# The third block's mixture of experts with two experts side by side

## The chip, the cores and the metric

The kernel runs on one core of a Trainium2 chip. The metric is the device time of one execution in microseconds (us). Three executions of the kernel before were timed; the median is the time before.

## What is computed

The reference is a network of four blocks, each of a cross attention, an attention or scan and a feed-forward part, on an x of 16 x 64 rows and 256 features. The kernel runs them as twelve layers, one after the other. The change concerns one, the feed-forward part of the block L2 (the third), whose layer is named `l2f`:

```
probs = softmax(x @ gate_w.T)            # 8 experts
topw, sel = top_k(probs, 2); topw /= sum(topw)
combine[t, e] = topw where e is selected, else 0
g, u = split(x @ w1[e].T)                # 176 and 176 columns
act = silu(g) * u
out = sum over e of combine[:, e] * (act @ w2[e].T)
```

Here x is the normalised stream and out is added to the stream. All eight experts are computed for every row; the weight of an expert that wasn't selected is zero. All of it is in fp32.

## The kernel before

`l2_ffn` (L3460) has the stream in SBUF as 8 tiles of 128 rows. A loop on each engine makes 4 trips, and each trip works on two tiles, called A and B here, whose programs are interleaved step by step (`in_turn`, L64): step i of A, then step i of B. There is no scheduler: the order of an engine's work is the order in which these programs are written, and semaphores carry the waits. Each tile has four PSUM banks: `hb` (two, for what the up-projection gives), `tb` (for transposed activations) and a bank for y.

A trip begins with a layer norm, its two transposes (L242), the gate's logits (L264, 8 columns), an exponential on POOL (L3497) and the choice of the two best on DVE (`Moe.route`, L613). POOL also splits a weight of the next layer into three bf16 parts after it, beside the experts (`ThreeParts.some`, L3609).

Then come the experts, in class `Moe` (L592). In `Moe.tensor` (L635) step i, 0 to 9, issues for each tile

- the up-projection of expert i (`project`, L264): 2 matmuls of 352 columns into `hb[i % 2]`, once DVE has read expert i-2 from it (signal `act_ready`);
- the transposes of expert i-1's 176 activations (L649), as parts of 128 and 48 columns, into `tb`, once DVE has made them and ACT has read the expert before from `tb` (`actT_ready`);
- the products of expert i-2 with `w_out` (L655), one matmul of 256 columns for each part, which contract over 128 and 48 rows and add up in y over all experts.

In `Moe.scalar` (L659) ACT computes the SiLU of the gate half (L665) and copies each transposed part to SBUF (L671). In `Moe.vector` (L673) DVE multiplies the other half by the SiLU and by the expert's weight (L680, into `act`, one of two buffers). `self.parts` holds the parts:

```
self.parts = [(a, min(P, inner - a)) for a in range(0, inner, P)]   # inner = 176
```

The trip ends with DVE's addition of y to the stream (L3518). The next trip's norm follows it.

The weights are loaded a layer ahead by SP (`l2_ffn_loads`, L3452), while layer `l2a` before runs. `w_out` comes in two transfers, rows 0 to 127 and 128 to 175 of every expert.

## Time and profile before

| | |
|---|---|
| median of 3 executions | 3598.69 us |
| lowest and highest | 3598.42 and 3602.27 us |
| the profiled execution | 3597.89 us |
| its span, from the first to the last instruction | 3596.1 us |
| mean granted TensorE clock | 0.876 |
| PE busy over the span | 2895.3 us (81%) |
| DVE, ACT, POOL busy | 2264.0, 1480.0, 588.4 us |

PE is TensorE's matmuls, PEld its weight loads, DVE VectorE, ACT ScalarE, POOL GpSimd, SP the engine that issues DMAs. "Idle before" is the time that the engine stood still before an instruction, with the one that ended the wait behind the arrow. An instruction can leave more than one record in the trace. PE's durations overlap at their ends, since matmuls are pipelined: what one costs in a full stream is the distance from its start to the start of the next. PEclk is the clock that TensorE was granted, as a share of 2.4 GHz, so 0.50 is 1.2 GHz.

### The profile page before, as it was taken

To read this page: it belongs to the slowest core of one execution; us is meant where nothing else is said; L and a number is where in the kernel's file an instruction comes from. 1 tells how busy PE (TensorE), PEld (TensorE's weight loads), DVE (VectorE), ACT (ScalarE), POOL (GpSimd) and SP (SyncE) were. 2 spreads that over 40 slices of the span, in tenths; PEclk is the share of its full clock that TensorE was granted. 3 is DMA by queue.
4 is the path that set the end of the run, shared out by engine and by line. 5 is a ranking of instruction groups with operands and counts; after the bars stand their busy time and mean duration, and the time that the engine had idled before them with its cause. 6 is when DMAs were issued, how large, how long until landed. Compare 5 with 4: busy or idle time off the path is not lost. (4 is left out here: it accounts for less than half of the span.)

```text
span 3596.1 us, 63959 instructions
## 1 busy us (share of the span) xinstructions
PE 2895.3 (81%) x24052; PEld 2020.0 (56%) x24100; DVE 2264.0 (63%) x4833; ACT 1480.0 (41%) x3050; POOL 588.4 (16%) x934
## 2 busy tenths in 40 slices
PE   6776699977867877749996869789999978787777
PEld 3333488776645555525654335456556557666666
DVE  6999644433658888776564832367777764444754
ACT  4899511112454645344442122155555533222222
POOL 5222100000002222111110032221211211111000
PEclk8899799988977778669998978899999989889788
DMA  4999900000010000010002040000000002000000
GB/s 121 198 204 206 215 0 0 0 24 6 15 53 3 3 2 3 2 75 6 9 9 72 2 140 23 3 4 3 3 6 3 3 27 116 1 0 0 1 1 12
DMA packets 316501, 141.44 MB, mean 39 GB/s; under 512 B 296221, under 2 KB 305950, under 8 KB 312613
## 3 DMA queue, kind: packets, MB, share of 16 engines
q1 hardware_dynamic: 308072, 138.46, 16.1%
q10 hardware_dynamic: 8256, 0.52, 0.2%
q8 instruction: 126, 2.06, 0.2%
q14 instruction: 47, 0.39, 0.0%
HBM read 67.65 MB, written 3.15 MB: 20 GB/s over the span
## 5 line engine op out<-in xcount | busy, mean ns | idle before, releaser
L1251 ACT ACTIVATE l0x_pb<-l0x_ex,l0x_neg_max,l0x_q_scale 128x2048 uint16<-128x2048 f32 x128 | 267.1, 2088 | 36.3 <-POOL l0x_neg_max L1354 25.0
L1150 PE MATMUL l0x_s_ps<-l0x_kT,l0x_qT 128*128 128x512 bf16 x466 | 167.0, 441 | 86.3 <-DVE l0x_ex L1449 42.8
L1447 DVE TENSOR_SCALAR_CACHE_REDUCE l0x_ex<-l0x_s_ps 128x1024 f32<-128x1024 f32 x128 | 156.3, 1221 | 15.2 <-PE l0x_s_ps L1150 14.5
L1449 DVE TENSOR_SCALAR_CACHE_REDUCE l0x_ex<-l0x_s_ps 128x1024 f32<-128x1024 f32 x128 | 156.2, 1221 | 0.0
L1150 PEld LDWEIGHTS l0x_s_ps<-l0x_kT,l0x_qT 128*128 128x128 bf16 x512 | 33.9, 102 | 155.6 <-DVE l0x_ex L1449 105.1
L264 PE MATMUL l3x_bank<-l3x_w_kv_x,l3x_ctxT 128*128 128x512 f32 x256 | 117.4, 601 | 4.4 <-ACT l3x_ctx_q L765 3.7
L2229 PEld LDWEIGHTS l1a_bank<-l1a_u,l1a_gm 64*64 64x64 f32 x2048 | 95.8, 193 | 17.7 <-issue 17.1
L1160 PEld LDWEIGHTS l0x_o_ps<-l0x_v,l0x_vT 128*128 128x128 f16 x2048 | 71.4, 99 | 60.6 <-DMA l0x_vT<-l0x_pb 30.3
L2229 PE MATMUL l1a_bank<-l1a_u,l1a_gm 64*64 64x8 f32 x2048 | 98.5, 235 | 7.7 <-DVE l1a_gm L2582 7.7
L264 PE MATMUL l2f_bank<-l2f_w,l2f_ln_yT 128*128 128x352 f32 x256 | 104.3, 542 | 0.0
L2221 PE MATMUL l1a_bank<-l1a_r,l1a_r 32*64 32x64 f32 x2048 | 70.9, 278 | 40.2 <-DVE l1a_r L2563 35.1
L2221 PEld LDWEIGHTS l1a_bank<-l1a_r,l1a_r 32*64 32x64 f32 x2048 | 65.0, 159 | 58.3 <-DVE l1a_r L2563 39.6
L680 DVE SCALAR_TENSOR_TENSOR l2f_moe_act<-l2f_bank,l2f_moe_cw,l2f_moe_sg 128x176 f32<-128x176 f32 x64 | 25.0, 400 | 115.5 <-ACT l2f_moe_sg L665 114.9
L710 PE MATMUL l3x_bank<-ident,l3x_rows 128*128 128x128 f32 x448 | 69.7, 289 | 33.3 <-ACT l3x_rows L758 33.3
L3714 PE MATMUL l3x_bank<-l3x_wproj,l3x_cat 128*128 128x256 bf16 x768 | 91.6, 277 | 4.1 <-DVE l3x_cat L3586 4.1
L2210 PE MATMUL l1a_bank<-l1a_steps,l1a_after 128*128 128x512 f32 x128 | 89.7, 790 | 0.0
L1160 PE MATMUL l0x_o_ps<-l0x_v,l0x_vT 128*128 128x16 f16 x2048 | 72.4, 171 | 18.9 <-DMA l0x_vT<-l0x_pb 18.6
L3714 PEld LDWEIGHTS l3x_bank<-l3x_wproj,l3x_cat 128*128 128x128 bf16 x768 | 74.4, 99 | 20.9 <-issue 6.6
L1351 POOL TENSOR_SCALAR l0x_mx<-l0x_low_max,l0x_high_max,l0x_q_neg 128x1 f32<-128x1 f32 x128 | 47.5, 371 | 216.2 <-DVE l0x_ex L1449 200.1
L4194 DVE TENSOR_TENSOR l3a_cur<-l3a_ret,l3a_bank 128x256 f32<-128x256 f32 x16 | 6.7, 422 | 117.7 <-PE l3a_bank L264 117.7
L710 PEld LDWEIGHTS l3x_bank<-ident,l3x_rows 128*128 128x128 f32 x448 | 51.0, 145 | 52.7 <-ACT l3x_rows L758 47.2
L655 PE MATMUL l2f_bank<-l2f_w,l2f_moe_actT 128*128 128x256 f32 (+1 forms) x256 | 78.6, 407 | 0.0
(756 smaller groups left out, 7774.9 us busy)
## 6 DMA issues: line engine op xcount, KB each, us to landing
l2f_wproj_raw<-in_L_xattn_wproj SPq DMA_DIRECT2D x2, 2048.0 KB, 12.8
l3a_w<-in_L_attn_W SPq DMA_DIRECT2D x4, 1024.0 KB, 10.6
l2f_w<-in_L_ffn_w SPq DMA_DIRECT2D x1, 2816.0 KB, 11.3
l0x_ex<-in_ctxT SPq DMA_DIRECT2D x8, 256.0 KB, 4.9
l0a_wq<-in_L_attn_W_Q SPq DMA_DIRECT2D x1, 2048.0 KB
l0a_wk<-in_L_attn_W_K SPq DMA_DIRECT2D x1, 2048.0 KB
l0x_vT<-l0x_pb SPq DMA_TRANSPOSE x128, 4.7
l0a_wv<-in_L_attn_W_V SPq DMA_DIRECT2D x1, 2048.0 KB, 7.9
```

The costliest lines, as they stand in the source:

```text
L264: ins = nc.tensor.matmul(out, wT(c), rhs(c), start=start and n == 0, stop=stop and n == chunks - 1)
L655: ins = nc.tensor.matmul(self.y, self.actT[0:w, e % 2, n, :], self.w_out[0:w, e, n, :], start=(e == 0 and n == 0), stop=(e == E - 1 and n ...
L710: ins = self.L.nc.tensor.transpose(self.banks[u][:, h * P:(h + 1) * P], self.rows[:, 4 * u + h, :], self.L.env.ident[:])
L1150: ins = mm(s_ps[:, j * 512:(j + 1) * 512], qT[:, h, :], kT[:, h // 2, j * 512:(j + 1) * 512], start=True, stop=True)
L1160: ins = mm(o_ps[:, h * HD:(h + 1) * HD], pt[:, h % 4, j * P:(j + 1) * P], vv[:, j, h * HD:(h + 1) * HD], start=j == 0, stop=j == KT - 1)
L1251: s.activation(pb[:, h % 4, :], ex[:, h % 4, :], ACT.Exp, scale=q_scale[:, h:h + 1], bias=nb[:, h:h + 1], accum_out=sums[:, h:h + 1]).then ...
L1447: v.tensor_scalar(ex[:, h % 4, 0:1024], s_ps[:, 0:1024], 1.0, None, ALU.mult, ALU.max, accum_out=low_max[:, h:h + 1]).then_inc(o.up(scores ...
L1449: v.tensor_scalar(ex[:, h % 4, 1024:2048], s_ps[:, 1024:2048], 1.0, None, ALU.mult, ALU.max, accum_out=high_max[:, h:h + 1]).then_inc(o.up ...
L2210: ins = mm(bank[4 + j][:], after[:], flat(steps_[:, 8 * j:8 * j + 8, :]), start=False, stop=True)
L2221: mm(out, r1[0][r, 8 * half + j, tok], r1[1][r, 8 * half + j, tok], start=True, stop=False)
L2229: ins = mm(bank[6][r, h * HP:(h + 1) * HP], gm[r, h, :], u[r, h * HP:(h + 1) * HP], start=True, stop=True)
L3714: ins = nc.tensor.matmul(y_bank, cat[:, 8 * (n % 2) + c, :], wproj[:, 8 * n + c, i, :], start=n % 2 == 0 and c + i == 0, stop=n % 2 == 1 a ...
```

## The change

Two experts with their 2 x 176 = 352 activations side by side are one row of 352 columns, cut into parts of 128, 128 and 96. DVE writes expert e into half e % 2 of a row of `act`, the buffers of `act` change with the pair instead of the expert. PE transposes at the even steps (2, 4, 6, 8) the pair that DVE has finished, three transposes for each tile, and multiplies by `w_out` at the odd steps (3, 5, 7, 9), three products for each tile. ACT copies the first two transposed parts in one instruction of 256 columns and the third in a second one. `w_out` is laid out on the host for pairs, three rows of 128 per pair with the last padded by zeros, and loaded in one transfer of 1,536 KB. The up-projections, SiLUs and DVE's products per expert are the same in number and size.

```diff
--- before.py
+++ after.py
@@ -597,17 +597,17 @@
         self.L, self.E, self.I, self.xT, self.w_in, self.w_out = L, experts, inner, xT, w_in, w_out
         self.hb, self.tb, self.y = banks[0:2], banks[2], y_bank
         self.fixed, self.factor = fixed, factor
-        self.parts = [(a, min(P, inner - a)) for a in range(0, inner, P)]
+        self.parts = [(a, min(P, 2 * inner - a)) for a in range(0, 2 * inner, P)]
         self.score = L.sb(f"{name}_score", [P, 8])
         self.top, self.idx = L.sb(f"{name}_top", [P, 8]), L.sb(f"{name}_idx", [P, 8], mybir.dt.uint32)
         self.idxf, self.iota = L.sb(f"{name}_idxf", [P, 8]), iota
         self.second, self.den = L.sb(f"{name}_second", [P, 8]), L.sb(f"{name}_den", [P, 1])
         self.cw = L.sb(f"{name}_cw", [P, 8 + fixed])
-        self.sg, self.act = L.sb(f"{name}_sg", [P, 2, inner]), L.sb(f"{name}_act", [P, 2, inner])
+        self.sg, self.act = L.sb(f"{name}_sg", [P, 2, inner]), L.sb(f"{name}_act", [P, 2, 2 * inner])
         self.actT = L.sb(f"{name}_actT", [P, 2, len(self.parts), P])
         E = experts
         self.hid_ps, self.silu = L.sig(f"{name}_hid_ps", E), L.sig(f"{name}_silu", E)
-        self.act_ready, self.actT_ps, self.actT_ready = L.sig(f"{name}_act_ready", E), L.sig(f"{name}_actT_ps", E), L.sig(f"{name}_actT_ready", E)
+        self.act_ready, self.actT_ps, self.actT_ready = L.sig(f"{name}_act_ready", E), L.sig(f"{name}_actT_ps", E // 2), L.sig(f"{name}_actT_ready", E // 2)
         self.y_ps = L.sig(f"{name}_y_ps")
 
     def route(self, o):
@@ -640,20 +640,20 @@
                 if i >= 2:
                     pe.wait_ge(self.act_ready.sem, self.act_ready.value(t, i - 1))
                 project(nc, self.hb[i % 2][:, 0:2 * I], lambda c: self.xT[:, c, :], lambda c: self.w_in[:, c, i * 2 * I:(i + 1) * 2 * I], DC).then_inc(self.hid_ps.sem, 1)
-            if 1 <= i <= E:
-                e = i - 1
-                pe.wait_ge(self.act_ready.sem, self.act_ready.value(t, e + 1))
-                if e:
-                    pe.wait_ge(self.actT_ready.sem, self.actT_ready.value(t, e))
+            if i >= 2 and i % 2 == 0:
+                pair = i // 2 - 1
+                pe.wait_ge(self.act_ready.sem, self.act_ready.value(t, 2 * pair + 2))
+                if pair:
+                    pe.wait_ge(self.actT_ready.sem, self.actT_ready.value(t, pair))
                 for n, (a, w) in enumerate(self.parts):
-                    ins = nc.tensor.transpose(self.tb[0:w, n * P:(n + 1) * P], self.act[:, e % 2, a:a + w], self.L.env.ident[:])
+                    ins = nc.tensor.transpose(self.tb[0:w, n * P:(n + 1) * P], self.act[:, pair % 2, a:a + w], self.L.env.ident[:])
                 ins.then_inc(self.actT_ps.sem, 1)
-            if i >= 2:
-                e = i - 2
-                pe.wait_ge(self.actT_ready.sem, self.actT_ready.value(t, e + 1))
+            if i >= 3 and i % 2:
+                pair = i // 2 - 1
+                pe.wait_ge(self.actT_ready.sem, self.actT_ready.value(t, pair + 1))
                 for n, (a, w) in enumerate(self.parts):
-                    ins = nc.tensor.matmul(self.y, self.actT[0:w, e % 2, n, :], self.w_out[0:w, e, n, :],
-                                           start=(e == 0 and n == 0), stop=(e == E - 1 and n == len(self.parts) - 1))
+                    ins = nc.tensor.matmul(self.y, self.actT[0:w, pair % 2, n, :], self.w_out[0:w, pair, n, :],
+                                           start=(pair == 0 and n == 0), stop=(2 * pair == E - 2 and n == len(self.parts) - 1))
         ins.then_inc(self.y_ps.sem, 1)
 
     def scalar(self, o):
@@ -663,12 +663,13 @@
             if i < self.E:
                 o.eng.wait_ge(self.hid_ps.sem, self.hid_ps.value(o.t, i + 1))
                 s.activation(self.sg[:, i % 2, :], self.hb[i % 2][:, 0:I], ACT.Silu).then_inc(o.up(self.silu), 1)
-            if 1 <= i <= self.E:
-                e = i - 1
-                o.eng.wait_ge(self.actT_ps.sem, self.actT_ps.value(o.t, e + 1))
-                for n, (a, w) in enumerate(self.parts):
-                    last = n == len(self.parts) - 1
-                    s.activation(self.actT[0:w, e % 2, n, :], self.tb[0:w, n * P:(n + 1) * P], ACT.Copy).then_inc(o.up(self.actT_ready if last else None), 1)
+            if i >= 2 and i % 2 == 0:
+                pair = i // 2 - 1
+                o.eng.wait_ge(self.actT_ps.sem, self.actT_ps.value(o.t, pair + 1))
+                whole_rows = len(self.parts) - 1
+                s.activation(flat(self.actT[:, pair % 2, 0:whole_rows, :]), self.tb[:, 0:whole_rows * P], ACT.Copy).then_inc(o.up(), 1)
+                w = self.parts[-1][1]
+                s.activation(self.actT[0:w, pair % 2, whole_rows, :], self.tb[0:w, whole_rows * P:(whole_rows + 1) * P], ACT.Copy).then_inc(o.up(self.actT_ready), 1)
 
     def vector(self, o):
         v, I = self.L.nc.vector, self.I
@@ -677,7 +678,7 @@
             if e >= self.E:
                 continue
             o.eng.wait_ge(self.silu.sem, self.silu.value(o.t, e + 1))
-            v.scalar_tensor_tensor(out=self.act[:, e % 2, :], in0=self.hb[e % 2][:, I:2 * I], scalar=self.cw[:, e:e + 1], in1=self.sg[:, e % 2, :],
+            v.scalar_tensor_tensor(out=self.act[:, e // 2 % 2, e % 2 * I:(e % 2 + 1) * I], in0=self.hb[e % 2][:, I:2 * I], scalar=self.cw[:, e:e + 1], in1=self.sg[:, e % 2, :],
                                      op0=ALU.mult, op1=ALU.mult).then_inc(o.up(self.act_ready), 1)
 
 
@@ -3446,15 +3447,14 @@
 
 def l2_ffn_weights(W):
     E, I = 8, 176
-    return (W.sb("w1", [P, DC, E * 2 * I]), W.sb("w2", [P, E, 2, D]), W.sb("gate_w", [P, DC, E]), W.sb("iota", [P, 8]))
+    return (W.sb("w1", [P, DC, E * 2 * I]), W.sb("w2", [P, E // 2, 3, D]), W.sb("gate_w", [P, DC, E]), W.sb("iota", [P, 8]))
 
 
 def l2_ffn_loads(sp, d, W, w1, w2, gate_w, iota):
     sp.dma_start(gate_w[:], d["L2_ffn_gate_w"]).then_inc(W.sem, W.loaded())
     sp.dma_start(iota[:], d["iota8"]).then_inc(W.sem, W.loaded())
     sp.dma_start(w1[:], d["L2_ffn_w1"]).then_inc(W.sem, W.loaded())
-    sp.dma_start(w2[:, :, 0, :], d["L2_ffn_w2a"]).then_inc(W.sem, W.loaded())
-    sp.dma_start(w2[0:176 - P, :, 1, :], d["L2_ffn_w2b"]).then_inc(W.sem, W.loaded())
+    sp.dma_start(w2[:], d["L2_ffn_w2"]).then_inc(W.sem, W.loaded())
 
 
 def l2_ffn(nc, env):
@@ -4753,8 +4753,9 @@
         f["L2_attn_" + n] = spread(i["L2_attn_" + n])
 
     f["L2_ffn_gate_w"], f["L2_ffn_w1"] = rows(i["L2_ffn_gate_w"].T), rows(i["L2_ffn_w1"].reshape(-1, D).T)
-    w2 = i["L2_ffn_w2"].transpose(2, 0, 1)
-    f["L2_ffn_w2a"], f["L2_ffn_w2b"] = np.ascontiguousarray(w2[:P]), np.ascontiguousarray(w2[P:])
+    w2 = np.zeros((4, 3 * P, D), np.float32)
+    w2[:, 0:2 * 176] = i["L2_ffn_w2"].transpose(0, 2, 1).reshape(4, 2 * 176, D)
+    f["L2_ffn_w2"] = np.ascontiguousarray(w2.reshape(4, 3, P, D).transpose(2, 0, 1, 3))
 
     g = lambda n: i["L3_xattn_" + n]
     for n in ("wq", "wk", "wv", "wqx", "w_kv_x", "wproj"):
```

PE at the start of a trip's experts (L264 the up-projection, x2 for one expert and tile; L649 a transpose; L655 a product with `w_out`; ISA and REGISTER_ALU rows set registers of a wait). Before:

```order
L264 MATMUL l2f_bank<-l2f_w,l2f_ln_yT 128x352 x6
L645 ISA
L649 MATMUL l2f_bank<-ident,l2f_moe_act 128x128
L649 MATMUL l2f_bank<-ident,l2f_moe_act 48x128
L264 MATMUL l2f_bank<-l2f_w,l2f_ln_yT 128x352 x2
L649 MATMUL l2f_bank<-ident,l2f_moe_act 128x128
L649 MATMUL l2f_bank<-ident,l2f_moe_act 48x128
L264 MATMUL l2f_bank<-l2f_w,l2f_ln_yT 128x352 x2
L645 REGISTER_ALU
L649 MATMUL l2f_bank<-ident,l2f_moe_act 128x128
L649 MATMUL l2f_bank<-ident,l2f_moe_act 48x128
L655 MATMUL l2f_bank<-l2f_w,l2f_moe_actT 128x256 x2
```

The same place after the change:

```order
L264 MATMUL l2f_bank<-l2f_w,l2f_ln_yT 128x352 x8
L641 ISA
L264 MATMUL l2f_bank<-l2f_w,l2f_ln_yT 128x352 x2
L645 REGISTER_ALU
L649 MATMUL l2f_bank<-ident,l2f_moe_act 128x128 x2
L649 MATMUL l2f_bank<-ident,l2f_moe_act 96x128
L264 MATMUL l2f_bank<-l2f_w,l2f_ln_yT 128x352 x2
L649 MATMUL l2f_bank<-ident,l2f_moe_act 128x128 x2
L649 MATMUL l2f_bank<-ident,l2f_moe_act 96x128
L264 MATMUL l2f_bank<-l2f_w,l2f_ln_yT 128x352 x2
L653 ISA
L655 MATMUL l2f_bank<-l2f_w,l2f_moe_actT 128x256 x3
```

Before, three up-projections (x6) stand ahead of the first wait for DVE, and the fourth, B's second, behind A's first transposes. Now four (x8) stand ahead of it, and six transposes of a step stand with two up-projections between products.

PE at the close of a trip, from B's last products of the step before on. Before:

```order
L655 MATMUL l2f_bank<-l2f_w,l2f_moe_actT 128x256 x2
L645 REGISTER_ALU
L649 MATMUL l2f_bank<-ident,l2f_moe_act 128x128
L649 MATMUL l2f_bank<-ident,l2f_moe_act 48x128
L655 MATMUL l2f_bank<-l2f_w,l2f_moe_actT 128x256 x2
L649 MATMUL l2f_bank<-ident,l2f_moe_act 128x128
L649 MATMUL l2f_bank<-ident,l2f_moe_act 48x128
L655 MATMUL l2f_bank<-l2f_w,l2f_moe_actT 128x256 x6
```

After the change:

```order
L655 MATMUL l2f_bank<-l2f_w,l2f_moe_actT 128x256 x3
L645 REGISTER_ALU
L649 MATMUL l2f_bank<-ident,l2f_moe_act 128x128 x2
L649 MATMUL l2f_bank<-ident,l2f_moe_act 96x128
L649 MATMUL l2f_bank<-ident,l2f_moe_act 128x128 x2
L649 MATMUL l2f_bank<-ident,l2f_moe_act 96x128
L653 REGISTER_ALU
L655 MATMUL l2f_bank<-l2f_w,l2f_moe_actT 128x256 x6
```

Before, the products of the expert before stand between a tile's last transposes and its last products. Now only the other tile's three transposes stand there.

## Rows read from the trace of the kernel before

**Rows 1.** Stretches of the expert stage: us, busy (records) per engine, PEclk, DMA, GB/s.

```profile
2157.75:2198.78 41.03, 41.03 (x148) 23.15 (x148) 6.19 (x16) 11.13 (x46) 5.77 (x4) 0.95 0.13 51
...
2169.41:2180.05 10.64, 10.64 (x42) 6.08 (x41) 1.60 (x4) 2.60 (x12) 0.00 (x0) 1.00 0.07 28
2090.00:2316.00 226.00, 197.38 (x688) 114.59 (x688) 65.83 (x192) 56.14 (x208) 69.81 (x56) 0.87 0.15 56
```

**Rows 2.** Groups by line and shape: records, busy us, mean ns, idle before.

```profile
L264 PE MATMUL l2f_bank<-l2f_w,l2f_ln_yT 128*128 128x352 f32 x256 | 104.3, 542 | 0.0
L655 PE MATMUL l2f_bank<-l2f_w,l2f_moe_actT 48*128 48x256 f32 x128 | 44.5, 428 | 0.0
L655 PE MATMUL l2f_bank<-l2f_w,l2f_moe_actT 128*128 128x256 f32 x128 | 39.0, 387 | 0.0
L649 PE MATMUL l2f_bank<-ident,l2f_moe_act 128*128 128x128 f32 x64 | 18.9, 295 | 13.9 <-DVE l2f_moe_act L680 13.9
```

**Rows 3.** Timeline of PE, second trip: start, duration, instructions, idle before.

```profile
2144.87 0.69 PE L242 MATMUL l2f_bank<-ident,l2f_ln_y 128*128 128x128 f32 x2 [0.25 <-DVE l2f_ln_y L213]
2145.35 1.77 PE L264 MATMUL l2f_bank<-l2f_gate_w,l2f_ln_yT 128*128 128x8 f32 x8
2146.97 6.20 PE L264 MATMUL l2f_bank<-l2f_w,l2f_ln_yT 128*128 128x352 f32 x12
2157.75 0.69 PE L649 MATMUL l2f_bank<-ident,l2f_moe_act 128*128 128x128 f32 x2 [4.58 <-DVE l2f_moe_act L680]
2158.23 2.55 PE L264 MATMUL l2f_bank<-l2f_w,l2f_ln_yT 128*128 128x352 f32 x4
...
2166.75 1.45 PE L264 MATMUL l2f_bank<-l2f_w,l2f_ln_yT 128*128 128x352 f32 x4
...
2168.26 1.22 PE L655 MATMUL l2f_bank<-l2f_w,l2f_moe_actT 128*128 128x256 f32 x4
2169.41 1.45 PE L264 MATMUL l2f_bank<-l2f_w,l2f_ln_yT 128*128 128x352 f32 x4
...
2193.34 0.44 PE L649 MATMUL l2f_bank<-ident,l2f_moe_act 128*128 128x128 f32 x2
...
2195.05 3.73 PE L655 MATMUL l2f_bank<-l2f_w,l2f_moe_actT 128*128 128x256 f32 x12
2202.09 0.69 PE L242 MATMUL l2f_bank<-ident,l2f_ln_y 128*128 128x128 f32 x2 [3.31 <-DVE l2f_ln_y L213]
```

**Rows 4.** Timeline of PE, first trip.

```profile
2103.35 1.35 PE L264 MATMUL l2f_bank<-l2f_w,l2f_ln_yT 128*128 128x352 f32 x4
2104.53 0.38 PE L649 MATMUL l2f_bank<-ident,l2f_moe_act 128*128 128x128 f32 x2
2104.75 1.22 PE L655 MATMUL l2f_bank<-l2f_w,l2f_moe_actT 128*128 128x256 f32 x4
```

**Rows 5.** Timeline of DVE, second trip.

```profile
2157.29 1.02 DVE L680 SCALAR_TENSOR_TENSOR l2f_moe_act<-l2f_bank,l2f_moe_cw,l2f_moe_sg 128x176 f32<-128x176 f32 x3
```

**Rows 6.** Timeline of ACT, second trip.

```profile
2144.65 0.39 ACT L251 ACTIVATE l2f_ln_yT<-l2f_bank 128x256 f32<-128x256 f32 x1 [5.52 <-PE l2f_bank L242]
...
2193.82 0.43 ACT L671 ACTIVATE l2f_moe_actT<-l2f_bank 128x128 f32<-128x128 f32 x2 [0.99 <-PE l2f_bank L649]
```

**Rows 7.** Timeline of the DMA issues on SP's queue.

```profile
1952.10 7.19 SPq L3457 DMA_DIRECT2D l2f_w<-in_L_ffn_w2b  x1
2065.27 1.72 SPq L3219 DMA_DIRECT2D l2a_turn_out<-l2a_res  x2
```

**Rows 8.** DMA issues by size, us to landing.

```profile
l2f_w<-in_L_ffn_w2b SPq DMA_DIRECT2D x1, 384.0 KB, 16.5
```

**Rows 9.** PE in single microseconds: busy (records), PEclk, DMA, GB/s.

```profile
2157.00:2158.00 1.00, 0.25 (x1) 0.50 0.00 0
...
2162.00:2163.00 1.00, 1.00 (x6) 0.96 0.00 0
...
2201.00:2202.00 1.00, 0.00 (x0) 0.50 0.00 0
```

## The prediction

> **What bounds the kernel here.** The change touches one stage of twelve, the mixture of experts of the third block, so the first view is the table of stretches over that stage. It lies between 2090 and 2316 us of the span; in these 226 us PE is busy 197.4, DVE 65.8, ACT 56.1, POOL 69.8 [rows 1]. Inside the steady part of one trip, 2169.41 to 2180.05, PE is busy 10.64 of 10.64 us at full granted clock, ACT 2.60 and DVE 1.60. PE sets the pace and nothing else is near it, so what PE no longer issues is worth its issue time.
>
> The second view, groups by line and shape, tells what PE issues [rows 2]. Each fp32 matmul of the source leaves two records, each transpose leaves one. So there are 128 up-projections (352 columns), 128 products with w_out (256 columns; half of them contract over 48 rows), and 128 transposes (half of 48 columns). The 48-row products are no cheaper than the 128-row ones, 428 ns against 387 a record. An expert of 176 columns pays for two full blocks: that is the waste the change goes for.
>
> The third view is PE's timeline. In the steady part one expert of one tile has a period of 2166.75 to 2169.41 = 2.66 us [rows 3]. Its pieces at full clock: two up-projections (call them **h**) 2103.35 to 2104.53 = 1.18, two transposes 2104.53 to 2104.75 = 0.22 [rows 4], so 0.11 each (**t**), and the two products take the rest, 2.66 - 1.18 - 0.22 = 1.26, so 0.63 each (**o**). These add up over a whole trip: from 2157.75 to 2198.78 the second trip issues 13 h, 32 t and 32 o, which is 15.34 + 3.52 + 20.16 = 39.0, and half of the 4.3 us that it spends at half clock (below) makes it 41.2; the stretch is 41.03 us [rows 1].
>
> **The change part by part.**
>
> *Fewer PE instructions.* A pair of experts had 4 transposes and 4 products per tile; it now has 3 and 3. With 8 tiles and 4 pairs, 32 t and 32 o go: 32 x 0.11 + 32 x 0.63 = 3.5 + 20.2 = **-23.7 us**. Bounds: an o in the mixed pattern could be as little as 1.15/2 = 0.575 (2168.26 to the next period at 2169.41), which makes it 21.9 in all. The up-projections and the SiLUs and DVE products per expert stay as they are.
>
> The new third transpose has 96 columns where the one removed had 48. The rows: at half clock a pair of one full and one 48-column transpose takes 2157.75 to 2158.23 = 0.48, and a pair of two full ones (the norm's) 2144.87 to 2145.35 = 0.48 [rows 3]. So the width of the loaded block doesn't count and three cost 0.33. The Trainium skill speaks against that ("TensorE: Matmul & The Clock Gate", section "LDWEIGHTS (loading the stationary operand)": the load's time goes by its columns). By that rule the pair's stationary columns, 352, are the same before and after, nothing is won on the transposes, and the sum would be 3.5 us smaller; the two 0.48 us intervals side with no such cost.
>
> *The short contraction.* The removed product is, in effect, a 48-row one. The Trainium skill ("TensorEngine Tiling (Array Packing)", section "When to Use Tiling") would have contractions of up to 64 rows run as two row tiles side by side, so by that rule a 48-row product might be half hidden and packing it into a full block would win little. Here the records of 48 rows aren't shorter [rows 2], and the closing run of 12 records, half of them 48-row, lasts 3.73 us [rows 3], which is 6 x 0.63 with nothing hidden.
>
> *Order at the start of a trip.* Before, the fourth up-projection (B's second expert) stood behind the transpose of A's first, which waits for DVE. Now four up-projections go out ahead of the first wait. In trips 2 to 4 PE waits there, 13.9 us in all [rows 2], in trip 2 4.58 us from 2153.2 to 2157.75 [rows 3]. The end of that wait is DVE's: it routes both tiles and starts its first expert product at 2157.29 [rows 5]; that chain hangs on the trip's norm, not on the up-projections, and doesn't move. So one h slides into the wait: -1.18 in each of three trips, **-3.5 us**. In trip 1 PE has no such wait and wins nothing. What is late next is still DVE's routing; the wait becomes about 3.4 us.
>
> *Waits inside a trip.* The transposes of a pair now need the second expert's product from DVE, the three w_out products need both ACT copies. Cover in the steady part: after A's transposes PE issues B's h (1.18), B's transposes (0.33) and A's next h (1.18), 2.7 us, while the two copies are done about 1.2 us after the first transpose (worked out below). And between the up-projection of a pair's second expert and that pair's transposes PE issues at least one tile's three products and more, 1.89 + 0.33, where now SiLU and DVE's product follow an up-projection within a period. Cost nothing. DVE and ACT have far more room than this, see their 1.60 and 2.60 of 10.64.
>
> *The close of a trip.* There the cover is gone: A's 3 transposes, B's 3, then A's products. The copies now start some 0.6 us after A's first transpose (0.48 before, 2193.34 to 2193.82 [rows 3, 6], plus one t); the 256-column copy takes 0.39 (the norm's copy of the same width) and the second adds about half of the 0.43 that two small ones span [rows 6]. So products can start about 1.2 us after A's first transpose, PE is done with B's at 0.66: a new wait of 0.5 us, four times, **+2.0 us** (between 0 and 1.2 each). B's copies are covered by A's three products (1.9 us).
>
> *The weight load.* Two transfers become one of 1,536 KB instead of 1,408. It is issued near 1952.10 and landed 16.5 us later [rows 7, 8]; first use is past 2100, and SP's next work comes at 2065. Cost nothing, even twice as long.
>
> *The clock.* PE's granted clock is 0.50 when PE restarts after the wait and comes back within 2162 [rows 9], 4.3 us after 2157.75, a loss of about 2.1 us per trip. The new wait of 3.4 us is nearly that between trips (3.31, until 2202.09 [rows 3]), during which the clock fell to 0.50 as well [rows 9]. So I leave the loss as it is. The other end is that the clock stays up: 3 x 2.1 = 6.3 us more.
>
> **The sum.** -23.7 - 3.5 + 2.0 = -25.2 us. The profiled execution took 3597.89 (span 3596.1 and 1.8 around it), 0.8 below the median of the three runs, which is no more than they differ. 3597.9 - 25.2 = 3572.7: I give **3573**. A measurement of this kernel tells about 0.2%, 7 us, from no change.
>
> **Rivals.**
> 1. *The clock stays up through the shorter wait.* For it: the wait shrinks by a quarter, and four up-projections instead of three run right before it. Against: the gap of 3.31 us lost it. Gives 3572.7 - 6.3 = **3566**. Chance 0.18.
> 2. *Part of the terms isn't there*: transposes priced by columns (+3.5), the moved h not hidden (+3.5), close of the trip at its upper end (+2.8), alone or two together: **3577 to 3582**. Chance 0.15.
> 3. *The 48-row products were all but hidden*, so that a full product costs more than a half of the pair: then 20 of the 25 us don't come, **3593**, which counts as no change. For it: the rule on tiling. Against: rows 2. Chance 0.03.
> 4. *Slower: the clock falls inside the trips.* Place: each of the four even steps, where six transposes now stand together at up-projections, and the new close. Price: a stretch like that after 2157.75, 2.1 us; at four per trip 16 x 2.1 = 34 us against 25 won: **3607**. It decides from three such falls per trip on (12 x 2.1 = 25). Against: there is no new gap over 0.5 us, and the present mix, transposes included, keeps 1.00 throughout the steady rows [rows 1]. Chance 0.02.
>
> The forecast has 0.62. Of these cases all but the last two are faster by over 0.2%: **faster 0.95, same 0.03, slower 0.02**. The range takes the forecast's own bounds (o at 0.575, the close between 0 and 1.2 us: 3571 to 3577), rival 1 up to 2 us beyond it for stages behind whose clock falls differently, and nearly all of rival 2: **3564 to 3581**.
>
> **What would show it.** Right: the stage ends 25 us earlier and the stages around it keep their length; L655 has 192 records instead of 256 and L649 96 instead of 128, of the same mean; a steady period of a pair and tile of 2 x 1.18 + 0.33 + 1.89 = 4.58 us instead of 5.32; PE's wait for the first expert product some 3.4 us, its end at the same distance from the norm; a wait of about 0.5 us for ACT's copy at each close. Wrong: a steady period above 4.8, waits for ACT or DVE inside it, a granted clock under 1.00 in the even steps, or a stage behind that changes by more than 3 us.

## The result and the profile after

The changed kernel takes 3551.9 us (median of four runs, 3549.84 to 3555.99), the kernel before 3600.35 in the same session (3598.42 to 3602.27): a ratio of 0.987, 95% interval 0.9856 to 0.9887. The forecast was 3573, with a range of 3564 to 3581. The sign was right, the gain of 25 us was little more than half of what came, and the measured time lies outside the range. Measured again later beside its successors (after_again, below), the changed kernel took 3556.01 against 3599.29, 43.3 us less; the difference between the gains of 48.5 and 43.3 us is not explained by anything in the stage.

| | before | after |
|---|---|---|
| profiled execution, us | 3597.89 | 3555.99 |
| span, us | 3596.1 | 3554.2 |
| expert stage, first norm transpose to that of the next stage, us | 231.22 | 188.53 |
| its trips, us | 51.89, 58.16, 58.10, 63.07 | 44.89, 46.89, 44.71, 52.04 |

In this pair of profiles the stage lost 42.7 us and the span 41.9: all of it went where the change is. That is also what the table of stretches says. Of the kernel before, with the stretches ahead of the stage, the stage, and what is behind it (us, busy us and records per engine, then PEclk):

```profile
0.00:2092.04 2092.04, 1630.92 (x16260) 1126.38 (x16309) 1413.21 (x2451) 923.12 (x1648) 312.61 (x546) 0.86 0.25 54
2092.04:2323.26 231.22, 197.38 (x689) 114.62 (x689) 68.10 (x202) 55.15 (x207) 70.44 (x58) 0.86 0.14 55
2323.26:3596.10 1272.84, 1066.98 (x7104) 778.95 (x7104) 782.67 (x2180) 501.75 (x1195) 205.39 (x331) 0.91 0.04 13
```

The same three stretches of the changed kernel:

```profile
0.00:2091.91 2091.91, 1649.33 (x16308) 1131.03 (x16308) 1412.71 (x2451) 922.81 (x1648) 313.09 (x546) 0.86 0.25 54
2091.91:2280.44 188.53, 153.88 (x593) 109.44 (x593) 67.75 (x202) 49.33 (x143) 70.51 (x58) 0.88 0.18 68
2280.44:3554.20 1273.76, 1069.71 (x7104) 781.41 (x7104) 781.73 (x2180) 501.04 (x1195) 205.63 (x331) 0.91 0.04 13
```

PE's busy time in the stage fell by 43.5 us, from 197.38 to 153.88, with 96 fewer records of it (64 of products, 32 of transposes). DVE and POOL did the same work as before. ACT copies in fewer instructions, 143 records for 207.

Groups by line and shape of the changed kernel, the rows that answer to [rows 2] (busy us, mean ns, idle before and its releaser):

```profile
L264 PE MATMUL l2f_bank<-l2f_w,l2f_ln_yT 128*128 128x352 f32 x256 | 97.2, 517 | 9.7 <-DVE l2f_moe_act L681 9.7
L655 PE MATMUL l2f_bank<-l2f_w,l2f_moe_actT 128*128 128x256 f32 x128 | 33.3, 382 | 1.2 <-ACT l2f_moe_actT L672 1.2
L655 PE MATMUL l2f_bank<-l2f_w,l2f_moe_actT 96*128 96x256 f32 x64 | 19.1, 379 | 0.0
L649 PE MATMUL l2f_bank<-ident,l2f_moe_act 128*128 128x128 f32 x64 | 12.6, 283 | 0.0
L649 PE MATMUL l2f_bank<-ident,l2f_moe_act 128*96 128x128 f32 x32 | 9.0, 281 | 0.0
```

The counts are as forecast, 192 and 96. But the products went from 44.5 + 39.0 = 83.5 us to 33.3 + 19.1 = 52.4, by 31.1, where a quarter of 83.5 is 20.9. The up-projections, all still there, are shorter too, 97.2 for 104.3. The wait for DVE is 9.7 us in three trips for 13.9, and a wait of 1.2 us for ACT is new, 0.3 at each close.

PE's timeline of the changed kernel, a steady part and the close of the second trip, answers to [rows 3] (start, duration, instructions, idle before):

```profile
2160.41 1.35 PE L264 MATMUL l2f_bank<-l2f_w,l2f_ln_yT 128*128 128x352 f32 x4
2161.59 0.49 PE L649 MATMUL l2f_bank<-ident,l2f_moe_act 128*128 128x128 f32 x3
2161.92 1.35 PE L264 MATMUL l2f_bank<-l2f_w,l2f_ln_yT 128*128 128x352 f32 x4
2163.11 0.49 PE L649 MATMUL l2f_bank<-ident,l2f_moe_act 128*128 128x128 f32 x3
2163.43 1.35 PE L264 MATMUL l2f_bank<-l2f_w,l2f_ln_yT 128*128 128x352 f32 x4
2164.62 1.46 PE L655 MATMUL l2f_bank<-l2f_w,l2f_moe_actT 128*128 128x256 f32 x6
2165.92 1.35 PE L264 MATMUL l2f_bank<-l2f_w,l2f_ln_yT 128*128 128x352 f32 x4
...
2168.40 1.35 PE L264 MATMUL l2f_bank<-l2f_w,l2f_ln_yT 128*128 128x352 f32 x4
...
2177.51 2.86 PE L655 MATMUL l2f_bank<-l2f_w,l2f_moe_actT 128*128 128x256 f32 x12 [0.31 <-ACT l2f_moe_actT L672]
```

From 2160.41 to 2168.40 both tiles go through one pair: 7.99 us for two, **3.99 for a pair and tile** where 4.58 was forecast and 5.32 was measured before. The up-projection is 1.18 as before and three transposes take 0.33, as forecast. Only the products differ: three of them take 2164.62 to 2165.92 = **1.30 us**, not 1.89. So one costs 0.43, not 0.63, and the products before cost more than that on average (1.26 for two).

### The profile page after: what moved, and what is told of

Same layout as the page of the kernel before. It is cut to its first block and busy times, and to the rows that moved or that the text cites. A ratio compares the mean times of both kernels' runs of the same rounds, so it can differ in the third digit from the quotient of the medians.

```text
span 3554.2 us, 63746 instructions
## 1 busy us (share of the span) xinstructions
PE 2872.9 (81%) x24004; PEld 2021.9 (57%) x24004; DVE 2262.2 (64%) x4833; ACT 1473.2 (41%) x2986; POOL 589.2 (17%) x934
## 5 line engine op out<-in xcount | busy, mean ns | idle before, releaser
L1151 PE MATMUL l0x_s_ps<-l0x_kT,l0x_qT 128*128 128x512 bf16 x512 | 177.3, 437 | 77.5 <-DVE l0x_ex L1450 41.1
L1151 PEld LDWEIGHTS l0x_s_ps<-l0x_kT,l0x_qT 128*128 128x128 bf16 x512 | 33.3, 101 | 156.6 <-DVE l0x_ex L1450 105.9
L264 PE MATMUL l3x_bank<-l3x_w_kv_x,l3x_ctxT 128*128 128x512 f32 x256 | 117.4, 601 | 4.4 <-ACT l3x_ctx_q L766 3.7
L2222 PE MATMUL l1a_bank<-l1a_r,l1a_r 32*64 32x64 f32 x2048 | 73.6, 288 | 44.4 <-DVE l1a_r L2564 40.9
L1161 PEld LDWEIGHTS l0x_o_ps<-l0x_v,l0x_vT 128*128 128x128 f16 x2048 | 71.0, 99 | 60.3 <-DMA l0x_vT<-l0x_pb 31.1
L264 PE MATMUL l2f_bank<-l2f_w,l2f_ln_yT 128*128 128x352 f32 x256 | 97.2, 517 | 9.7 <-DVE l2f_moe_act L681 9.7
L2223 PE MATMUL l1a_bank<-l1a_r,l1a_r 32*64 32x64 f32 x2048 | 73.9, 264 | 9.2 <-issue 9.2
L264 PEld LDWEIGHTS l3x_bank<-l3x_w_kv_x,l3x_ctxT 128*128 128x128 f32 x256 | 46.0, 190 | 55.8 <-issue 51.4
```

Of the source, the lines that this page charges most:

```text
L264: ins = nc.tensor.matmul(out, wT(c), rhs(c), start=start and n == 0, stop=stop and n == chunks - 1)
L1151: ins = mm(s_ps[:, j * 512:(j + 1) * 512], qT[:, h, :], kT[:, h // 2, j * 512:(j + 1) * 512], start=True, stop=True)
L1161: ins = mm(o_ps[:, h * HD:(h + 1) * HD], pt[:, h % 4, j * P:(j + 1) * P], vv[:, j, h * HD:(h + 1) * HD], start=j == 0, stop=j == KT - 1)
L2222: mm(out, r1[0][r, 8 * half + j, tok], r1[1][r, 8 * half + j, tok], start=True, stop=False)
L2223: ins = mm(out, r2[0][r, 8 * half + j, tok], r2[1][r, 8 * half + j, tok], start=False, stop=True)
```

## The experiments

Each ratio is against the kernel before, measured in the same session on the same chip: rows48, rows64, rows128 and double48 in one session, rows96, after48, after_wait and after_early in a second, the last three rows of the table in a third. Beside the median, each kernel's profile gives the length of the expert stage (from the first norm transpose to that of the next stage), which is steadier than the whole time: the rest of the span varied by some us from one profile to the next with nothing changed there. It comes from one execution each. The changed kernel's two profiles gave 188.53 and 186.92, so a difference of 1 or 2 us between two stages tells nothing by itself.

| kernel | median us | ratio, 95% interval | stage us |
|---|---|---|---|
| before | 3597.88, 3598.43 and 3599.29 (three sessions) | | 231.22 |
| rows48 | 3599.63 | 1.0000, 0.9991 to 1.001 | 230.95 |
| rows64 | 3598.6 | 1.0005, 0.9995 to 1.0014 | 231.48 |
| rows96 | 3575.25 | 0.9943, 0.9926 to 0.9961 | 207.59 |
| rows128 | 3578.14 | 0.9941, 0.9924 to 0.9958 | 206.29 |
| double48 | 3627.79 | 1.0083, 1.0066 to 1.01 | 258.48 |
| after48 | 3570.18 | 0.9929, 0.9904 to 0.9953 | 196.14 |
| after_wait | 3563.54 | 0.9907, 0.9891 to 0.9924 | 195.15 |
| after_early | 3558.11 | 0.9887, 0.9868 to 0.9906 | 189.71 |
| after_later | 3542.49 | 0.9849, 0.9834 to 0.9863 | 174.76 |
| after_both | 3540.63 | 0.9836, 0.9819 to 0.9853 | 171.39 |
| after_again | 3556.01 | 0.9885, 0.9868 to 0.9902 | 186.92 |

Theory 1: a product over 48 rows between products over 128 costs more than its own time, because the weight loads don't run ahead over the change of rows. Theory 2: products simply got cheaper in longer runs of their kind (six records instead of four), whatever their rows.

### The same kernel before, with other rows in the second product

PE gets the same instructions as in the kernel before, but the second product of an expert contracts over K rows, those beyond 48 being zeros in both operands (rows48 is the control: the zeroing, and no other rows). The weights of the second product are loaded with K rows instead of 48, and ACT waits once for the zeroing; both are left out of the extract, as is everything behind `...`.

```diff
                 for n, (a, w) in enumerate(self.parts):
+                    w = P if n == 0 else ROWS_OF_SECOND
                     ins = nc.tensor.matmul(self.y, self.actT[0:w, e % 2, n, :], self.w_out[0:w, e, n, :],
...
         @block.gpsimd
         def _(pool):
+            for tile in tiles:
+                nc.gpsimd.memset(tile["moe"].actT[:, :, 1, :], 0.0).then_inc(tile["moe"].cleared.sem, 1)
...
```

**rows48.** 

> Control for the runs on rows: the kernel before, with a zeroed buffer for the second transposed part (two small memsets on POOL ahead of the stage's loop) and nothing else changed. All theories: within 1 us of the kernel before, w_out products (L655 of before) at 1.26 us per expert and tile.

**rows128.** 

> The kernel before, but the second product of every expert contracts over 128 rows, of which the last 80 are zeros on both sides, instead of 48. Same number of instructions. Theory 1 (going from a product over 128 rows to one over 48 and back costs 0.2 us each time, since the next weights aren't loaded ahead): two products take 0.86 us instead of 1.26, 64 experts and tiles x 0.40 = 26 us faster. Theory 2 (the prediction's: a product costs 0.63 us whatever its rows, and the extra gain comes from elsewhere): no change.

**rows64.** 

> As rows128, but over 64 rows. Theory 1, with two row settings and the border at 64: no change against the kernel before (1.26 us for two products). Theory 1 with a cost that goes by how unlike the row counts are: between, some 5 us faster. Theory 2: no change.

**rows96.** 

> As rows128, but the second product contracts over 96 rows. Theory 1 with the border above 64: the same gain as rows128 (about 20 us). A cost by the distance of the row counts: some third of the 1.26 - 0.86 us stays, 13 us faster.

PE's timeline of rows128, one expert of one tile:

```profile
2168.29 1.03 PE L660 MATMUL l2f_bank<-l2f_w,l2f_moe_actT 128*128 128x256 f32 x4
2169.15 1.35 PE L264 MATMUL l2f_bank<-l2f_w,l2f_ln_yT 128*128 128x352 f32 x4
2170.34 0.38 PE L653 MATMUL l2f_bank<-ident,l2f_moe_act 128*128 128x128 f32 x2
2170.56 1.03 PE L660 MATMUL l2f_bank<-l2f_w,l2f_moe_actT 128*128 128x256 f32 x4
```

The same of rows64:

```profile
2166.06 1.22 PE L660 MATMUL l2f_bank<-l2f_w,l2f_moe_actT 128*128 128x256 f32 x4
2167.22 1.45 PE L264 MATMUL l2f_bank<-l2f_w,l2f_ln_yT 128*128 128x352 f32 x4
...
2168.72 1.22 PE L660 MATMUL l2f_bank<-l2f_w,l2f_moe_actT 128*128 128x256 f32 x4
```

With 128 rows the period is 2168.29 to 2170.56 = 2.27 us instead of 2.66: **more rows, less time**. Of the 0.39, 0.30 us sit between the products' start and the next up-projection's (0.86 for 1.16), and 0.09 in the up-projection itself (1.19 for 1.28). With 64 rows the period is 2.66, as with 48; with 96 it is 2.27, as with 128. 64 experts and tiles by 0.39 are 25.0 us; the stage of rows128 is 24.9 shorter and that of rows96 23.6. Padding to 96 rows gained as much as to 128, so the surplus does not go by how far the row counts lie apart. The median of the whole fell less, by 19.7 and 23.2; the stretch behind the stage was 3 to 5 us longer in those profiles (1277.8 and 1276.0 against 1272.8), for which I have no cause. Theory 2 is excluded: here the runs of records have the same length as before, and the time still falls.

### The short product twice

```diff
...
-                                           start=(e == 0 and n == 0), stop=(e == E - 1 and n == len(self.parts) - 1))
+                                           start=(e == 0 and n == 0), stop=False)
+                ins = nc.tensor.matmul(self.y, self.actT[0:w, e % 2, n, :], self.w_out[0:w, e, n, :], start=False, stop=(e == E - 1))
```

**double48.** 

> The kernel before, with each 48-row product issued twice in a row (the second adds the same once more, so the output holds those 48 columns' share twice). Theory 1 (the change of rows costs, not the 48-row product): 64 x 0.43 = 27 us slower. Theory 2 (0.63 each): 40 us slower. Theory 3 (a 48-row product is slow in itself, 0.83 us): 53 us slower.

```profile
2169.30 1.22 PE L655 MATMUL l2f_bank<-l2f_w,l2f_moe_actT 128*128 128x256 f32 x4
2170.37 0.59 PE L657 MATMUL l2f_bank<-l2f_w,l2f_moe_actT 48*128 48x256 f32 x2
2170.89 1.45 PE L264 MATMUL l2f_bank<-l2f_w,l2f_ln_yT 128*128 128x352 f32 x4
2172.18 0.38 PE L649 MATMUL l2f_bank<-ident,l2f_moe_act 128*128 128x128 f32 x2
2172.39 1.22 PE L655 MATMUL l2f_bank<-l2f_w,l2f_moe_actT 128*128 128x256 f32 x4
```

The period is 2169.30 to 2172.39 = 3.09 us, 0.43 more than 2.66. A second 48-row product right behind the first costs what a full one costs. So the price is not in the short product but in the **change** from full rows to short ones and back: the two changes cost 0.39 together. The starts of PE's single records in the kernel before divide it: 2168.26, 2168.48, 2168.79, 2169.11, 2169.41 and 2169.81 (two of the full product, two of the short one, two of the up-projection). The distances are 0.22, 0.31, 0.32, 0.30 and 0.40, where a stream of full rows has 0.22 behind a product's record and 0.29 behind an up-projection's. That is 0.2 for the change to 48 rows and 0.2 for the change back. The stage grew by 27.3 us; 64 x 0.43 is 27.5.

### The change with a short third product

```diff
...
                 for n, (a, w) in enumerate(self.parts):
+                    w = P if n < 2 else 48
                     ins = nc.tensor.matmul(self.y, self.actT[0:w, pair % 2, n, :], self.w_out[0:w, pair, n, :],
...
```

**after48.** 

> The changed kernel, with the third product of a pair contracting over 48 of its 96 rows (48 rows of every second expert are left out, for the time only). Theory 1: 32 x 0.40 = 13 us slower than the changed kernel, three products take 1.7 us instead of 1.3. Theory 2: no change against it.

```profile
2159.75 1.65 PE L656 MATMUL l2f_bank<-l2f_w,l2f_moe_actT 128*128 128x256 f32 x6
2161.33 1.45 PE L264 MATMUL l2f_bank<-l2f_w,l2f_ln_yT 128*128 128x352 f32 x4
2162.62 0.49 PE L649 MATMUL l2f_bank<-ident,l2f_moe_act 128*128 128x128 f32 x3
```

The three products now take 2159.75 to 2161.33 = 1.58 us instead of 1.30, and the up-projection behind them 1.29 instead of 1.18: 0.39 again, in the changed kernel too. The stage grew by 7.6 us and not by 32 x 0.39 = 12.5. Of the difference, 3.0 is the gap behind trip 1, 3.50 us instead of 6.47, because trip 1 is now long enough to run into POOL's late split only a little (below). The other 1.9 lies in trip 4, which grew by 1.4 us instead of 3.1: there PE waited 2.94 us and the clock stayed at 1.00, while in the changed kernel it waited 3.27 and the clock was at 0.50 for 3.4 us.

### The wait put back ahead of the fourth up-projection

```diff
...
+            if i == 1:
+                pe.wait_ge(self.act_ready.sem, self.act_ready.value(t, 1))
...
```

**after_wait.** 

> The changed kernel, with a wait for the tile's first expert product put back ahead of B's second up-projection, where the kernel before had it. If moving that up-projection into the wait is worth what the prediction says: 3 x 1.2 = 3.5 us slower than the changed kernel, all of it in trips 2 to 4 (more where PE runs at half clock then, up to 3 x 2.4 = 7 us). Rival (the wait would have been hidden anyway): no change.

PE's waits at the start of trips 2 to 4 in this kernel:

```profile
2152.99 5.06 PE L264 MATMUL l2f_bank<-l2f_w,l2f_ln_yT 128*128 128x352 f32 x8 [4.18 <-DVE l2f_moe_act L683]
2201.89 4.33 PE L264 MATMUL l2f_bank<-l2f_w,l2f_ln_yT 128*128 128x352 f32 x8 [4.74 <-DVE l2f_moe_act L683]
2249.96 4.33 PE L264 MATMUL l2f_bank<-l2f_w,l2f_ln_yT 128*128 128x352 f32 x8 [4.88 <-DVE l2f_moe_act L683]
```

Against 3.63, 2.82 and 3.27 in the changed kernel these are 4.1 us more in all, and the stage is 6.6 longer (8.2 against the second profile of the changed kernel): the moved up-projection, and behind the longer wait more work at half clock. The two up-projections of each row above last 5.06 and 4.33 us, where two at full clock take 2 x 1.18 = 2.36 from start to start. How the 6.6 divides between the two was not measured.

### What holds up the trips now: POOL

POOL's timeline of the changed kernel, around the gap behind trip 1:

```profile
2122.17 1.04 POOL L3616 CAST l3x_wproj<-l2f_wproj_raw 128x1024 bf16<-128x1024 f32 x1 [23.45 <-DMA l2f_wproj_raw<-in_L_xattn_wproj]
...
2133.20 2.12 POOL L3622 TENSOR_TENSOR l3x_wproj<-l2f_wproj_raw,l3x_wproj 128x1024 bf16<-128x1024 f32 x1
2135.40 0.19 POOL L231 TENSOR_TENSOR l2f_ln_ve<-l2f_ln_mv,eps 128x1 f32<-128x1 f32 x1
...
2144.57 2.13 POOL L3618 TENSOR_TENSOR l2f_wproj_raw<-l2f_wproj_raw,l3x_wproj 128x1024 f32<-128x1024 f32 x1
2146.76 1.05 POOL L3620 CAST l3x_wproj<-l2f_wproj_raw 128x1024 bf16<-128x1024 f32 x1
2147.89 2.12 POOL L3622 TENSOR_TENSOR l3x_wproj<-l2f_wproj_raw,l3x_wproj 128x1024 bf16<-128x1024 f32 x1
```

POOL splits a weight of the next stage into parts (L3616 to L3622) between its own small steps of the norm and the routing. The first share waits for a transfer until 2122.17 and ends at 2135.3. Before, trip 1's last product ended later than that, at 2140.6; now it ends at 2130.3, and the next norm (L231) stands in POOL's queue behind the split. The gap between trips 1 and 2 is 6.47 us where it was 3.33.

DVE's timeline of the changed kernel, the second half of trip 2's routing:

```profile
2144.69 2.03 DVE L627 TENSOR_SCALAR l2f_moe_cw<-l2f_iota,l2f_moe_idxf,l2f_moe_top 128x8 f32<-128x8 f32 x1
2146.64 0.28 DVE L628 TENSOR_SCALAR l2f_moe_second<-l2f_iota,l2f_moe_idxf,l2f_moe_top 128x8 f32<-128x8 f32 x1
2146.95 0.88 DVE L630 TENSOR_TENSOR l2f_moe_cw<-l2f_moe_cw,l2f_moe_second 128x8 f32<-128x8 f32 x1
2147.87 2.17 DVE L632 TENSOR_SCALAR l2f_moe_cw<-l2f_moe_cw,l2f_moe_den 128x8 f32<-128x8 f32 x1
```

For the first tile, just ahead of this and with no share of the split beside it, L627, L630 and L632 take 0.27, 0.17 and 0.23 us. Here, on the same 128x8 elements, they take 2.03, 0.88 and 2.17, and each ends with POOL's instruction that ran beside it: 2146.72 and 2146.70, 2147.83 and 2147.81, 2150.04 and 2150.01. DVE isn't slowed in proportion, it is held until POOL's instruction is over. The Trainium skill says that in "SBUF — State Buffer", section "Who interferes with whom": DVE, in certain kinds of instruction, and POOL share a pair of ports that one of them holds for a whole instruction, while the other blocks. The trace agrees, by the three pairs of ends above. I had read that stretch of DVE only at its end [rows 5].

So it is POOL, through DVE, that would make the wait of PE at the start of trips 2 to 4. Two edits test it: load the raw weight earlier, and let POOL split only once the routing is done.

```diff
...
+            wproj.load_half(sp, d, 0)
             load_next(sp, env)
-            wproj.load(sp, d)
+            wproj.load_half(sp, d, 1)
...
```

**after_early** (this edit alone). 

> The changed kernel, with the first half of the next layer's wproj loaded ahead of that layer's other weights instead of behind them. POOL then splits it early in the first trip and is free when the second trip's norm needs it. If POOL's late split is what makes the first gap between trips 6.5 us instead of 3.3: 3.2 us faster than the changed kernel, gap 3.3. Rival: POOL's split now slows DVE's routing in the first trip, as it does in the others, and PE waits there some 3 us: no change.

No gain: a stage of 189.71 us against 188.53 and 186.92, and a ratio of 0.9887 against the 0.9885 of after_again. The first gap went back to 3.34, and POOL's first share now fell beside the routing of trip 1, where PE had not waited before:

```profile
2110.48 1.76 PE L264 MATMUL l2f_bank<-l2f_w,l2f_ln_yT 128*128 128x352 f32 x4 [3.36 <-DVE l2f_moe_act L681]
```

L627, L630 and L632 took 2.03, 0.88 and 2.17 us there, the same three numbers. The same collision, moved.

```diff
...
                 in_turn(*(tile["gpsimd"](pool, t) for tile in tiles))
+                routed = tiles[1]["moe"].act_ready
+                pool.wait_ge(routed.sem, routed.value(t, 1))
                 wproj.some(pool, t // 2, 2 * (t % 2))
...
```

**after_later** (this edit alone). 

> The changed kernel, with POOL waiting for DVE's first expert product of tile B before it starts to split wproj in each trip. If POOL's fp32 operations are what stretches DVE's routing (2.0, 0.9 and 2.2 us instead of 0.3, 0.2 and 0.2): the three stretched operations go back to those durations, PE's wait of some 3 us in trips 2 to 4 goes, 10 us faster than the changed kernel. Rival (the stretch has another cause, or PE then waits for something else): no change. The first gap between trips stays at 6.5 us.

**after_both** (both). 

> The changed kernel with both, the early load of wproj and the later split. Both waits should go then, each cure being what the other lacked: the first gap is 3.3 us, no trip waits for the routing, 13 us faster than the changed kernel. If the early load costs something else: as after_later.

**after_again** (the changed kernel, beside them). 

> The changed kernel once more beside the two, for a comparison on one chip. All theories: as it was, 1.3% faster than the kernel before, stage 188.5 us long from its first transpose to the next layer's.

Groups of after_both (busy us, mean ns, idle before):

```profile
L264 PE MATMUL l2f_bank<-l2f_w,l2f_ln_yT 128*128 128x352 f32 x256 | 93.2, 501 | 0.0
...
L627 DVE TENSOR_SCALAR l2f_moe_cw<-l2f_iota,l2f_moe_idxf,l2f_moe_top 128x8 f32<-128x8 f32 x8 | 2.2, 273 | 0.0
L632 DVE TENSOR_SCALAR l2f_moe_cw<-l2f_moe_cw,l2f_moe_den 128x8 f32<-128x8 f32 x8 | 1.8, 231 | 0.3
```

The routing steps are back at a mean of 0.27 and 0.23 us over all trips (0.93 and 0.96 in the changed kernel), and PE's wait for DVE is gone, 0.0 for 9.7. So the wait was POOL's doing. In the changed kernel of the same session, after_again, the three waits were 3.08, 3.49 and 2.60, 9.2 in all; after_later's stage is 12.2 us shorter than that one's. Of the other 3.0 us, 0.4 is the first gap (5.52 for 5.92); the fall of the clock behind the wait of 3.49 us, 3.4 us long, is gone too. The rest was not taken apart. after_both also shortens the first gap, from 5.92 to 3.33, and its stage is 15.5 shorter. POOL's split costs it as much as ever (70.5 us busy in both) and still ends in time. **after_both is the fastest version**: 3540.63 us, a ratio of 0.9836 where the change alone has 0.9885 in the same session. By the median it can't be told from after_later (0.9849, the intervals overlap); its stage is 3.4 us shorter. Both gained more than expected, 13.5 and 15.4 us for 10 and 13.

## Why the prediction was right in sign and wrong in size

*The step that failed is the price of a product*: "the two products take the rest, 2.66 - 1.18 - 0.22 = 1.26, so 0.63 each (o)". The 1.26 was a sum over two unlike things: a full-row product of 0.43 and a 48-row one of 0.83, two changes of rows included. Halving it is harmless only if what is removed is an average product. The change removes both 48-row products of a pair and adds one of 96 rows, which runs like a full one: per pair and tile 4 products in 2.52 us become 3 in 1.30. That is -1.22, not -0.63, and 32 of them are **-39.0 us where the sum had -20.2**. That is 18.8 us, more than the whole miss of the stage (42.7 for 25.2 is 17.5). The error is of size, in the largest term; that PE's issue time sets the pace and that what is no longer issued is won was right.

*Could it be seen in the trace before?* The records said 428 ns against 387 [rows 2], which I read as "no cheaper"; that small surplus can't show the price, since records overlap and their durations aren't distances between starts. The prediction also took the up-projection, 1.18 us, from a place ahead of all products [rows 4]; behind them its four records last 1.45 us and not 1.35 [rows 3], a sign that the products cost something beyond their own time. A view that I didn't print shows it best, the timeline of PE's weight loads in the kernel before:

```profile
2168.15 0.30 PEld L655 LDWEIGHTS l2f_bank<-l2f_w,l2f_moe_actT 128*128 128x128 f32 x2
2168.78 0.29 PEld L655 LDWEIGHTS l2f_bank<-l2f_w,l2f_moe_actT 48*128 48x128 f32 x2 [0.33 <-issue]
2169.41 0.89 PEld L264 LDWEIGHTS l2f_bank<-l2f_w,l2f_ln_yT 128*128 128x128 f32 x4 [0.33 <-issue]
```

The loader stands still for 0.33 us ahead of the first load of a short product and again ahead of the full load behind it. In the changed kernel it doesn't:

```profile
2163.32 0.89 PEld L264 LDWEIGHTS l2f_bank<-l2f_w,l2f_ln_yT 128*128 128x128 f32 x4
2164.32 1.35 PEld L655 LDWEIGHTS l2f_bank<-l2f_w,l2f_moe_actT 128*128 128x128 f32 x6
2165.70 1.00 PEld L264 LDWEIGHTS l2f_bank<-l2f_w,l2f_ln_yT 128*128 128x128 f32 x4
```

Between full rows a load starts within 0.01 us of the start of the matmul before it, and so is done ahead of its own; at the change to 48 rows the matmul before it starts at 2168.48 and the load only at 2168.78. The runs with other row counts say the same (groups of rows64 and rows96, the loads of the second product):

```profile
L660 PEld LDWEIGHTS l2f_bank<-l2f_w,l2f_moe_actT 64*128 64x128 f32 x128 | 18.8, 184 | 21.2 <-issue 21.2
L660 PEld LDWEIGHTS l2f_bank<-l2f_w,l2f_moe_actT 96*128 96x128 f32 x128 | 24.4, 191 | 3.3
```

With 64 rows the loader idles 21.2 us ahead of 64 products, 0.33 each, as with 48; with 96 rows 3.3 us in all. In double48 the idle time is ahead of the first short product alone. Why the loads wait at that change no run shows. The prediction bounded the term below only ("an o in the mixed pattern could be as little as 1.15/2 = 0.575"); a bound above, the two unlike products priced apart, was never set, and so the range missed.

*Rival 3*, that the 48-row products were all but hidden, was the opposite of the truth: one between full ones costs about twice a full one (0.83 us for 0.43). The Trainium skill, on which it leaned ("TensorEngine Tiling (Array Packing)", section "When to Use Tiling"), gives contractions of up to 64 rows two row tiles. The trace shows no saving from that for a short product in one stream with full ones.

*The transposes*: right. Three take 0.33 us, 96 columns cost what 48 did. The loads themselves are shorter for fewer columns (mean 147 ns for 128, 131 for 96, 108 for 48), but that doesn't show in the distance between starts.

*The moved up-projection*: right. 3.5 was forecast; PE's waits fell by 4.2 us, and undoing the move alone cost the stage 6.6, more than the 3.5 and within the 3.5 to 7 expected for work at half clock.

*The close of a trip*: right. The profile shows an idle time of 0.31 us each, but the price is a distance between starts: from A's first transpose to the first product 2176.39 to 2177.51 = 1.12 us, of which six transposes are 0.66. That leaves 0.46 for 0.5 forecast, 1.8 in all for 2.0.

*The weight load*: nothing, as forecast. The one transfer of 1,536 KB landed after 14.4 us, more than 100 us ahead of its use.

*The clock*: forecast unchanged, and it wasn't the main thing. In trips 2 and 4 it was at 0.50 for 3.4 us behind the wait, back 3.9 us after PE's restart in trip 2 (4.3 before), and after the 2.82 us wait of trip 3 it never fell. Rival 1 was true of one trip of three. Rival 4 was not: 1.00 from 2160.41 to 2168.40, and no fall inside a trip.

*Missed*: POOL as a gate. I looked for what would be late next at DVE and ACT inside a trip, not for what POOL's queue holds at the end of a shorter trip 1: +3.1 us. It is a consequence of the larger gain: the split ends at 2135.3 in both kernels, and the norm behind trip 1, which wanted POOL at 2142.5 before, would have wanted it at 2137.1 by my sum for a trip (-5.4) and did want it near 2132.2. The margin was 1.8 us, and I had not looked at it.

*The sum again*, with the measured prices: 32 x (1.22 + 0.11) = -42.6, the up-projection -3.5, the close +1.8, the first gap +3.1: -41.2 us, against -42.7 in the stage. Trip by trip, these prices give the changes of trips 1, 2 and 4 (-7.0, -11.3 and -11.0 us) within 0.4; trip 3, whose clock stayed up, is 2.0 us shorter than they say, which is what the prediction had one such fall cost (2.1).

## What to carry to other kernels

A mean over unlike instructions prices nothing that removes only one kind: take the distance from start to start for each kind, and where records overlap look at the weight loads' own timeline for idle time. In a stream of full-row fp32 matmuls a single product over 48 or 64 rows costs twice a full one here, so try padding it with zeros to 96 or 128 rows before thinking of anything cleverer (that alone was 24 us of the stage's 43). And when an engine on the path waits for small DVE instructions, look at what POOL runs beside them: holding back POOL's bulk work until the routing was done brought 13.5 us more for one wait.

## What the runs showed of the hardware that I had not expected

- Two fp32 products of 256 columns, 128 rows and then K rows, between full-row matmuls: the period they stand in is 2.66 us for K = 48 and 64, 2.27 for K = 96 and 128. The border lies between 64 and 96. A second 48-row product in a row adds 0.43, as a full one does; the surplus of 0.4 belongs to the pair of changes, and where it is paid the weight loads wait 0.33 us twice.
- DVE instructions of 0.27, 0.17 and 0.23 us took 2.03, 0.88 and 2.17 beside POOL's fp32 work on 128x1024, each until POOL's instruction was over, in the same three durations wherever the two met. L622, a cast of 128x8, was held as well: 0.32 us instead of 0.17, from 2144.20 to 2144.52, where POOL's L3616 ends at 2144.49. L617, L620 and L625 of the same routing took 0.16 to 0.17 us beside POOL's work as they do alone. Which kinds of instruction are held was not tried.
- After PE's idle stretches of 2.60, 2.82 and 3.08 us at the start of a trip the granted clock stayed at 1.00; after 3.27, 3.49 and 3.63 us it went to 0.50 for 3.4 us, beginning 1.2, 0.7 and 0.5 us behind the restart (the six waits of the two profiles of the changed kernel).
